# Preparing the expert weights W1 and W2 on ScalarE and VectorE beside the groups of nodes, instead of ahead of them with GpSimd

## What is computed

```python
x = x + layernorm(x) @ W                       # W: the table of edge weights
z = layernorm(x);  xn = layernorm(z) * gamma + beta
top_vals, top_idx = top_k(xn @ Wr + br, 2);  w = softmax(top_vals)
y_e = gelu(xn @ W1[e] + b1[e]) @ W2[e] + b2[e] # 8 experts, hidden 512
out = x + sum over the two chosen e of w_e * y_e
```

## Time and profile before

| | us |
|---|---|
| median of 3 runs (1061.28 to 1064.53) | 1061.4 |
| the profiled execution | 1061.05 |
| its span | 1059.3 |
| TensorE busy in the span | 900.6 (85%) |
| VectorE, ScalarE, GpSimd busy | 753.9, 633.8, 627.9 |
| GpSimd's scatters to slots, 196 of 978 ns | 191.6 |

### The profile page before, as it was taken

How to read it: one execution, slowest core, us unless ns; L and a number is a source line. 1 busy time by engine, 2 the same in 40 slices (tenths; PEclk the granted TensorE clock), 3 DMA queues, 4 the chain that set the end, 5 groups by cost and what they waited for, 6 DMA issues and landing times. The chain is left out here.

```text
span 1059.3 us, 25594 instructions
## 1 busy us (share of the span) xinstructions
PE 900.6 (85%) x6756; PEld 840.9 (79%) x6757; DVE 753.9 (71%) x2315; ACT 633.8 (60%) x1325; POOL 627.9 (59%) x490
## 2 busy tenths in 40 slices
PE   2583889898886029999999999999999999999992
PEld 1123777787775029999999999999999999999992
DVE  6985798999973507777777777777777777777761
ACT  2254666667662006776776776676676676677661
POOL 3664077777777743475565665665666564656653
PEclk9696899889986559999999999999999999999996
DMA  5055376766734533455544644544544554544542
GB/s 159 22 158 168 87 220 200 232 200 221 240 140 159 178 127 76 81 90 86 93 80 79 101 80 81 95 83 81 97 82 81 89 90 80 96 83 81 91 70 30
DMA packets 96231, 121.47 MB, mean 115 GB/s; under 512 B 15256, under 2 KB 73792, under 8 KB 96060
## 3 DMA queue, kind: packets, MB, share of 16 engines
q0 software_dynamic: 39904, 53.56, 29.0%
q1 hardware_dynamic: 55976, 66.58, 21.7%
q10 hardware_dynamic: 308, 0.85, 0.3%
HBM read 51.94 MB, written 69.00 MB: 114 GB/s over the span
## 5 line engine op out<-in xcount | busy, mean ns | idle before, releaser
L578 POOL DMA_INDIRECT out_dram<-ysb,yid x210 | 379.9, 1809 | 285.8 <-ACT ysb L1349 136.0
L749 PE MATMUL psum<-xh,w1s 128*128 128x256 f32 x1680 | 310.9, 285 | 0.0
L749 PEld LDWEIGHTS psum<-xh,w1s 128*128 128x128 f32 x1680 | 257.1, 189 | 0.0
L562 POOL DMA_INDIRECT slots<-arena_z,pos x196 | 191.6, 978 | 89.9 <-issue 59.1
L762 PE MATMUL psum<-w2h,hl 128*128 x840 | 237.5, 283 | 0.0
L762 PE MATMUL psum<-w2l,hh 128*128 x840 | 237.3, 283 | 0.0
L762 PE MATMUL psum<-w2h,hh 128*128 x840 | 237.2, 282 | 0.0
L749 PE MATMUL psum<-xl,w1s 128*128 128x256 f32 x840 | 235.2, 280 | 0.0
L1164 DVE TENSOR_TENSOR hl<-hact,hh 128x512 fp32r<-128x512 f32 x210 | 145.8, 694 | 87.9 <-ACT hh L1211 87.6
L1211 ACT ACTIVATE xh<-psum 128x512 fp32r<-128x512 f32 x105 | 62.7, 597 | 222.2 <-PE psum L736 222.2
L1332 ACT ACTIVATE hact<-psum,b1T 128x256 f32<-128x256 f32 x420 | 174.6, 467 | 14.3 <-PE psum L749 2.8
(11 more groups left out here) (187 smaller groups left out, 1119.9 us busy)
## 6 DMA issues: line engine op xcount, KB each, us to landing
zin<-slots SPq DMA_DIRECT2D x105, 260.0 KB
arena_x<-in_x_dram SPq DMA_DIRECT2D x14, 512.0 KB, 5.7
out_dram<-arena_s SPq DMA_DIRECT2D x14, 512.0 KB, 3.4
arena_z<-in_L_ffn_W_dram SPq DMA_DIRECT2D x24, 256.0 KB, 2.9
arena_x<-in_x_dram SPq DMA_DIRECT2D x13, 384.0 KB, 4.6
out_dram<-arena_s SPq DMA_DIRECT2D x13, 384.0 KB
out_dram<-ysb,yid POOLq DMA_INDIRECT x210, 4.2
slots<-arena_z,pos POOLq DMA_INDIRECT x196
```

Source lines behind the costliest of these rows:

```text
L562: pool.indirect_dma_start(slots[:, :], bass.IndirectOffsetOnAxis(ap=pos[b][0:n, k, s:s + 1], axis=0), zg[b][0:n, s, :], None).then_inc(sen ...
L578: pool.indirect_dma_start(out[:, :], bass.IndirectOffsetOnAxis(ap=yid[u % MB][:, n:n + 1], axis=0), ysb[u % YB][:, n, :], None, compute_op ...
L749: last = nc.tensor.matmul(bank[2 + 2 * b + q][:, m * PAIR:(m + 1) * PAIR], w1s[b][:, w, k, hb * P:(hb + 1) * P], xs[b][:, k * PAIR:(k + 1) ...
```

## The change

W2 is now prepared first (pieces 0 to 15), then W1 (16 to 31). Pieces 0 to 11 are prepared beside the groups with two buffers of their own (`wst_new`), pieces 12 to 31 with five buffers (three lie in the space of the normalized x). ScalarE writes the high part (`high`) at the end of its groups 2 to 13, VectorE the low part (`low`) at the end of its groups 3 to 13 and behind; for W1 one instruction scales by gamma and subtracts. GpSimd has no part in it. `turn_over(g)` on SP is followed by `load_w(g)`, which waits until the buffer's last user has its low part. TensorE's product of beta with W1 moves behind the last group, as columns of a transposed bias, so the way of the bias through DRAM goes.

```diff
+WHOLE = 2 * PIECES
+BESIDE = 12
+FIRST_BESIDE = 2
+WBUFS = 5
+MIDDLE = PIECES + WBUFS
+WBUF = [n % 2 if n < BESIDE else (n - BESIDE) % WBUFS for n in range(WHOLE)]
...
+def last_user(n):
+
+    return max((m for m in range(n) if WBUF[m] == WBUF[n]), default=-1)
...
+            def load_w(n):
+
+                m = last_user(n)
+                if m >= 0:
+                    sp.wait_ge(w_low, m + 1)
+                    if m >= PIECES:
+                        sp.wait_ge(w_read, m - PIECES + 1)
...
-            for b in range(SB):
-                load_w1(0, b)
             for h in range(2):
                 load_x(0, 0, h)
...
+            for n in range(2):
+                load_w(n)
             for g in range(2, GROUPS - 3):
                 turn_over(g, g % 2)
+                load_w(g)
             turn_over(GROUPS - 3, 1, full=False)
+            load_w(GROUPS - 3)
             turn_over(GROUPS - 2, 0, load=False)
+            sp.wait_ge(xT_mm, NP * GROUPS)
+            for n in range(BESIDE, BESIDE + WBUFS):
+                load_w(n)
...
+            for n in range(BESIDE + WBUFS, WHOLE):
+                load_w(n)
...
-            def low(ready, c, target, full, high):
-                wait_apart(pool, ready, c, pool_passed)
-                pool.tensor_tensor(target, full, high, ALU.subtract).then_inc(w_low, 1)
...
-                    if j < len(late):
-                        bias_product(late[j])
...
+            for n in range(PIECES):
+                e, k = n // KD, n % KD
+                pe.wait_ge(stage_in[WBUF[PIECES + n]], 16 * turn_of(PIECES + n) + 16)
+                for hb in range(KH):
+                    last = nc.tensor.matmul(bank[7][:, KH * e + hb:KH * e + hb + 1], wst[WBUF[PIECES + n]][:, hb * P:(hb + 1) * P], bet[:, k:k + 1],
+                                            start=(n == 0 and hb == 0), stop=(n == PIECES - 1 and hb == KH - 1))
+                last.then_inc(w_read, 1)
...
+            def low(n):
+
+                e, k = (n % PIECES) // KD, n % KD
+                dve.wait_ge(w_high, n + 1)
+                if n < PIECES:
+                    v.tensor_tensor(w2l[:, e, 2 * k:2 * k + 2, :].rearrange("p k d -> p (k d)"), wst[WBUF[n]],
+                                    w2h[:, e, 2 * k:2 * k + 2, :].rearrange("p k d -> p (k d)").bitcast(F32), ALU.subtract).then_inc(w_low, 1)
...
+                if g > FIRST_BESIDE:
+                    low(g - FIRST_BESIDE - 1)
...
+            for n in range(BESIDE - 1, MIDDLE):
+                low(n)
             for _ in route(GROUPS - 1, (GROUPS - 1) % RZ, full=False):
...
+            for n in range(MIDDLE, WHOLE):
+                low(n)
+            dve.wait_ge(w_read, PIECES)
+            dve.wait_ge(b1_in, 16)
+            v.tensor_tensor(b1T[:, :], bank[7][:, 0:E * KH], b1raw[:, :], ALU.add).then_inc(bias_ready, 1)
...
             act.wait_ge(table_ready, 1)
-            act.wait_ge(w_low, PIECES)
             group(0, 0, z_side=False, older=False)
-            high2(HALF, E // 2)
-            act.wait_ge(w_low, 2 * PIECES)
             group(1, 1, older=False)
             for g in range(2, GROUPS):
                 group(g, g % 2)
+                high(g - FIRST_BESIDE)
             group(GROUPS, 0, x_side=False)
+            for n in range(BESIDE, MIDDLE):
+                high(n)
             exp_gap(GROUPS - 1)
+            for n in range(MIDDLE, WHOLE):
+                high(n)
```

More of the change, by code:

```diff
@@ L66, in used, with turn_of @@
     return NP * g + max(q - 1, 0)
+def turn_of(n):
+    return sum(WBUF[m] == WBUF[n] for m in range(n))
+def last_user(n):
+    return max((m for m in range(n) if WBUF[m] == WBUF[n]), default=-1)
 def wait_apart(engine, sem, value, apart):
@@ L217, in build @@
         table = front("table", [P, KD, D], F32)
-        b1row = front("b1row", [E, H], F32)
+        wst_new = front("wst_new", [P, 2 * H], F32)
         XG = G * D
@@ L287, in build @@
         table_ready = sem("table_ready")
-        stage_in = [sem(f"stage_in{i}") for i in range(SB)]
+        stage_in = [sem(f"stage_in{i}") for i in range(WBUFS)]
         w_high = sem("w_high")
-        w_product = sem("w_product")
         w_low = sem("w_low")
         w_read = sem("w_read")
-        bias_added = sem("bias_added")
-        bias_out = sem("bias_out")
         b1_in = sem("b1_in")
+        bias_ready = sem("bias_ready")
         b2_in = sem("b2_in")
@@ L393, in _ @@
             w2_pieces = W2.rearrange("(i u) (k p) d -> i u k p d", u=2, p=P)
[L395 to L400, removed]
-            for b in range(SB):
-                load_w1(0, b)
+            def load_w(n):
[4 more added lines that the diff above has]
+                        sp.wait_ge(w_read, m - PIECES + 1)
+                i, u, k = (n % PIECES) // 4, (n // 2) % 2, n % 2
+                if n < PIECES:
+                    sp.dma_start(wst[WBUF[n]].rearrange("p (k d) -> p k d", k=2),
+                                 w2_pieces[i:i + 1, u, 2 * k:2 * k + 2, :, :].rearrange("a k p d -> p (a k) d")).then_inc(stage_in[WBUF[n]], 16)
+                else:
+                    sp.dma_start(wst[WBUF[n]], w1_pieces[i:i + 1, u, k, :, :].rearrange("a p h -> p (a h)")).then_inc(stage_in[WBUF[n]], 16)
             for h in range(2):
                 load_x(0, 0, h)
[L405 to L421, removed]
             sp.wait_ge(table_ready, 1)
@@ L458, in _ @@
                 sp.wait_ge(sent[b], 16 * 2 * G * len(range(b, GROUPS, RZ)))
+            sp.wait_ge(w_low, WHOLE)
+            sp.wait_ge(w_read, PIECES)
             def pair_row(i, u):
@@ L536, in _ @@
             fetch(0)
[L537 to L548, removed]
             pool.wait_ge(n_max_ready, 1)
@@ L618, in _, with picks @@
             last.then_inc(lbias_mm, 1)
-            def bias_product(e):
-                for k in range(KD):
-                    n = KD * e + k
-                    pe.wait_ge(stage_in[n % SB], 16 * (n // SB) + 16)
-                    nc.tensor.matmul(bank[7][0:E, :], bet_e[:, k, e, :], stage[n % SB], start=(n == 0), stop=(n == PIECES - 1)).then_inc(w_read, 1)
-            for e in range(EARLY):
-                bias_product(e)
             pe.wait_ge(n_max_ready, 1)
             most = pe.value_load(n_max[0:1, 0:1], min_val=0, max_val=ECT)
-            def picks(r, late=()):
+            def picks(r):
                 pe.wait_ge(diag_ready, r + 1)
@@ L645, in picks @@
                     last.then_inc(new_ready, 1)
-            picks(0, late=range(EARLY, E))
+            picks(0)
             with pe.If(most > PICK):
@@ L1364, in _ @@
             act.wait_ge(tables_ready, 1)
-            act.wait_ge(b1_in, 16)
+            act.wait_ge(bias_ready, 1)
             es = experts(nc, act, tile_i[:, 0, :], 0)
```

58 lines of the change are left out of this document (18 added, 40 removed).

## The result

The changed kernel takes 1140.2 us (median of 6 runs, 1134.2 to 1145.5) against 1061.9 of the kernel before measured beside it (1060.3 to 1064.5): ratio 1.073, 95% interval 1.071 to 1.075. The forecast was 1118 us with a range of 1097 to 1142: the sign and the mechanism came as foretold, the size lies at the upper edge of the range. The profiled execution took 1138.4 us with a span of 1136.7; its first transposes of the pairs start at 468.61, 78.6 us later than before, and the pairs behind them take as long as before (668.1 us against 669.2). So all of the loss is ahead of them. (All times are those of undisturbed executions; one of the last experiment's four, 1206.8 us at a mean granted clock of 0.72 where the others have 0.92, is left out.)

A forecast was written before the change was run, and what follows sets the result against it. GpSimd's scatters were taken to bound the start of the pairs, and after the change SP's held-back x loads: nine groups of 24.8 us and the tail put first transposes at 447.1 against 390.06; 1061.05 + 57.0 = 1118 us, range 1097 to 1142.

The forecast's parts named there:

- the circle: Groups 4 to 12: SP's load_w waits for VectorE's last low, x loads stand behind it, VectorE's next group needs x.
- The front: Ahead of the scatters: 6.8 (small VectorE step) + 3.7 (picks) + 4.7 (group 0) bring place(0) 15.2 us sooner.
- The period: Each of groups 4 to 12: 15.6 + 0.6 + 7.6 + 1.0 = 24.8 us, bounds 23.1 and 27.4.
- The stall: VectorE standing still for the late loads of x in groups 4 to 12: 7.6 us a group.
- The clock: TensorE returns from idling at its lower clock, and VectorE waits for one slow edge product: 1.0 us a group.
- The work: VectorE's own steps in a group: 15.6 us, plus 0.6 for the added low, 16.2 in all.
- Rival C: TensorE stays at its lower clock and scatters slow the loads: 27.4 us a group, 1141 us; chance 0.10.
- The end of the groups: Group 13 takes 20.2 us, then lows 11 to 20 and routing to the last positions 24.0 (bounds 19 and 27).
- Behind the last positions: From last positions to first transposes: load 31 about 15 us, fillers to 29, then row and zin, 33.5 (30 to 36).
- A: Rival, groups: transfers come before VectorE stands still, GpSimd bounds until the tail, pairs start 11.7 us early: 1049 us; chance 0.05.
- B: Rival, groups: the second half of x lands with the first, 23.1 us a group, 1103 us; chance 0.12.
- D: Rival, tail: fillers come in time and the pairs start behind the last scatters: 1110 us; chance 0.08.

The follow-up runs named there:

- the last experiment: Changed kernel with the low ahead of the additions, plus the tail's early bias products and moved fillers: 1053.6 us, ratio 0.989 against the kernel before.

## Where the prediction was right and where not

**What bounds, and the sign: right.** The waits came where they were foretold: at the start of groups 4 to 12 for x, and once more ahead of the fifth statistics. With the circle open the scatters end the chain again, and the pairs never changed.

**The front: 15.2 foretold, 16.2 measured.** Timeline of VectorE in the changed kernel, and GpSimd's first scatter:

```profile
38.86 0.17 DVE L903 TENSOR_SCALAR alive<-beaten 128x8 f32<-128x8 f32 x1
...
44.16 0.69 DVE L921 TENSOR_TENSOR arena_x<-psum,arena_x 128x512 int32<-128x512 f32 x1
...
65.97 0.72 DVE L924 COPY_PREDICATED table<-arena_x,psum 128x512 f32<-128x512 int32 x1
...
117.58 1.00 POOL L549 DMA_INDIRECT slots<-arena_z,pos  x1 [82.08 <-DVE pos L1024]
```

The step of 7.03 us takes 0.17: 6.9 us. The eight picks take 22.5 us (44.16 to 66.69) instead of 27.5: 4.9, above the 3.7 taken and a little above the bound of 4.5. Some 4 us came in group 0 and the rest between. The scatters start at 117.58 instead of 133.77. Group 3 with its low ended at 146.22; 146.2 was forecast.

**The period: mechanism right, size 24.8 against 27.2.** Measured from the waits above: 8.5 us for x (76.3 / 9), 2.0 for TensorE (16.2 + 1.8, by 9), and 16.7 of work. The prediction had 7.6, 1.0 and 16.2. Three terms were too small:
- The stall by 0.9. The first half of x came 7.6 us behind the low in the turn shown, not 6.6: from its issue it took 6.6 us and not 5.7, with W, x1 out and scatters beside it. The second came 10.3 behind instead of 9.2.
- The clock by 1.0. I let VectorE wait for one slow edge product and took 1.0 of its 1.6; it waits nearly twice in a group (15 times in nine).
- The work by 0.5. 15.6 was the shortest group of before, not a mean; with no wait but that for x (14 products) it is 16.6.

Over the nine groups that makes 21.8 us, the whole miss of 20.4 (1138.4 against 1118) and a little more; the end of the groups gave 3.2 back, the time behind the positions added 2.9, and the pairs took 1.1 less. Rival C has nearly the same period (27.4): its price for the clock came (1.8 foretold, 2.0 measured), its stall did not (9.4 and 8.5), nor did scatters throughout, since GpSimd paused; and its work was short by the same 0.5. That the measured time lies beside C's 1141 is luck in part. The range is tighter above than its own words: 6 us beyond C would have been 1147 and not 1142, and two of the six runs lie above 1142 (1142.2 and 1145.5).

**The end of the groups: 44.2 foretold, 41.0 measured.** Group 13 took 17.6 instead of 20.2: from its first addition to its end with the low 13.1 us and not 15.2; the group of before from which I took that the earlier trace rows was longer. The lows and the last positions took 23.4 (24.0 foretold, though its terms, 18 and 6.4, add up to 24.4).

**Behind the last positions: 33.5 foretold, 36.4 measured, and a wrong step.** I let load 31 wait for lows. Timeline of TensorE and SP:

```profile
432.36 1.85 PE L707 MATMUL psum<-bet,arena_x 128*128 128x1 f32 x8
...
454.55 5.26 PE L707 MATMUL psum<-bet,arena_x 128*128 128x1 f32 x24
...
468.61 1.11 PE L721 MATMUL psum<-ident,zin 128*128 128x128 f32 x4 [8.81 <-DMA zin<-slots]
...
447.93 3.74 SPq L415 DMA_DIRECT2D arena_x<-in_L_ffn_W_dram  x3
451.73 0.43 SPq L448 DMA_DIRECT2D out_dram<-filler  x1
...
454.27 8.76 SPq L453 DMA_DIRECT2D slots<-filler  x8
465.91 1.50 SPq L469 DMA_DIRECT2D zin<-slots  x2
```

TensorE's 16 bias products of eight rows run from 432.36 to 459.8 without a pause, 1.71 us each, and each frees one buffer: load 31 waits for the eleventh and goes out at 451.3, 19 us behind the positions instead of 15; low(26), which I had it wait for, was done at 447.7, 15.5 behind them. That the products bind is shown by SP's eleven waits on them, and by the run with five of them early: there load 31 goes out 15.7 us behind the positions (447.01), and the pairs start 2.8 us sooner. I had named the product among what frees a buffer and priced only the low. What follows load 31 was taken at 18.5 us and measured 17.3, which hid part of this: the terms named add up to 17.6 (29 and 0.8 and 2.8, less 15), and the 0.9 left for "the issue between" has no row, nor does a run show it.

**The rivals.** A (faster, 1049) needed the transfers in time; opened in three ways the circle gives 1050.7 to 1052.4, so its number was near once its condition was made true, but by luck in part: what ended the chain was GpSimd and not its tail. B did not come: the second half of x landed 2.7 us behind the first. Nor did D: the pairs start 16.1 us behind the last scatter, which ended at 452.54, where 5.3 follow it when the fillers are in time.

**The price of a low for GpSimd: taken as nothing, wrong.** I inferred it from VectorE's 694 ns beside scatters; but it is the scatter that waits. Counted over the 196 scatters of the timeline with x ahead of W, the 27 that a low overlapped took 1.17 us in the mean, the others 0.98, while some 50 beside an addition with one input in PSUM took 0.97. The Trainium skill ("SBUF — State Buffer", section "Who interferes with whom") has this contention of a VectorE instruction with two SBUF inputs and a GpSimd instruction that reads SBUF. The trace agrees on the kind; its size is 3.1 us for the eleven lows in the groups and 5.8 in all, not the 11 that I had worked out from it. In the changed kernel GpSimd's pauses hide it.

## What to carry to other kernels

Before a load is put behind a wait on an engine that issues others' loads, ask who releases the wait and whether that engine's next step needs what stands behind: if so, each turn costs a full transfer (here 8.5 us of stall, and 2 more through TensorE's clock), whatever slack the other engines have. Open such a circle at any of its points (order, place of the release, issuing engine), and then look at what the chain ends in next. A price read from one engine's duration says nothing on the engine beside it.

## What the hardware showed beyond this

Four lows in a row behind the tables held up one scatter in the kernel with x ahead of W: the scatter at 352.60 took 3.05 us and not 0.97, while the lows ran from 352.09 to 354.80. In five other profiles one scatter beside such a row of four or five lows took 2.76 to 4.00 us. The scatter at 370.56 there took 2.37 us beside two casts of 2.37 in all at 370.44 (timeline of VectorE):

```profile
370.44 2.37 DVE L1157 CAST w1s<-w 128x2048 fp32r x2 [1.06 <-issue]
```

Products with one column are not cheap: the 128 of the bias took 27.4 us, 0.21 each. TensorE worked through them without a pause; the loads of their weights (PEld) were busy 27.4 of the 28 us from 432 to 460, and the granted clock stayed at 0.50. What they take at 1.00 no run shows.
